# A three-layer graph network: the slot numbers of all node tiles scattered by GpSimd, and the second count of edges on TensorE taken out

## The reference

```python
h, residual = x, 0.0
for Wl, bl, Wr, g, b in params:
    s = segment_sum(h[src], dst, num_segments=N_NODES)
    cnt = segment_sum(ones, dst, num_segments=N_NODES)
    h = residual + (s / maximum(cnt, 1)) @ Wl.T + bl + h @ Wr.T
    h = prelu(layer_norm(h, g, b), a_prelu)
    residual = h
out = layernorm(x + h)
```

## Time and profile before

| what | value |
|---|---|
| median of 3 runs | 2023.56 us (2023.55 to 2024.12) |
| profiled execution, its own time | 2023.93 us |
| its span | 2022.1 us |
| mean granted TensorE clock | 0.993 of full speed |
| PE, DVE, ACT, POOL busy | 98%, 79%, 60%, 46% |
| data moved | 387.69 MB, mean 192 GB/s |

### The profile page before, as it was taken

One profiled execution on the slowest core, in us unless ns is written; L12 is line 12 of the kernel. 1 busy time (PEld: TensorE's weight loads), 2 busy tenths in 40 slices (PEclk: granted clock), 3 DMA queues, 4 the chain that ended last, 5 costly groups with the idle time before them and its releaser, 6 DMA issues. The chain is left out here.

```text
span 2022.1 us, 30522 instructions
## 1 busy us (share of the span) xinstructions
PE 1978.4 (98%) x10207; PEld 1659.0 (82%) x10207; DVE 1597.5 (79%) x2598; ACT 1221.7 (60%) x2667; POOL 926.7 (46%) x885
## 2 busy tenths in 40 slices
PE   8999999999999999999999999999999999999993
PEld 7888888888888888888888888887788888888882
DVE  7778777777777677777777777779999988888884
ACT  6865554554444455444444444458887777777774
POOL 3666656555565312332222333214555555555554
PEclk9999999999999999999999999999999999999997
DMA  6667667666666555544444444456666666656652
GB/s 209 226 232 258 215 219 233 221 208 214 204 204 207 161 162 183 170 146 152 146 145 151 157 156 144 138 173 216 221 230 217 211 212 213 209 203 218 214 183 92
DMA packets 181075, 387.69 MB, mean 192 GB/s; under 512 B 20117, under 2 KB 20562, under 8 KB 180918
## 3 DMA queue, kind: packets, MB, share of 16 engines
q1 hardware_dynamic: 142358, 272.06, 39.7%
q0 software_dynamic: 38560, 113.67, 17.3%
HBM read 221.07 MB, written 164.79 MB: 191 GB/s over the span
## 5 line engine op out<-in xcount | busy, mean ns | idle before, releaser
L411 PE MATMUL ps_z<-w_hi,hT_hi 128*128 128x512 f32 x1884 | 762.9, 405 | 5.7 <-ACT ps_z L553 4.9
L411 PE MATMUL ps_z<-w_hi,hT_lo 128*128 128x512 f32 x1884 | 738.6, 392 | 0.0
L411 PE MATMUL ps_z<-w_lo,hT_hi 128*128 128x512 f32 x1884 | 737.8, 392 | 0.0
L690 POOL TENSOR_TENSOR rstd<-veps,minus_half 128x2 f32<-128x2 f32 (+1 forms) x240 | 241.6, 1007 | 876.1 <-ACT veps L543 876.0
L790 DVE TENSOR_TENSOR hT_lo<-ps_t,hT_hi 128x1024 fp32r<-128x1024 f32 (+1 forms) x237 | 288.0, 1215 | 320.3 <-ACT hT_hi L524 317.6
L553 ACT COPY ps_z<-bias_rows 128x512 f32<-128x512 f32 x471 | 276.7, 588 | 346.5 <-DVE y L801 334.7
L533 ACT ACTIVATE junk<-ps_z 128x512 f32<-128x512 f32 x471 | 278.6, 592 | 322.3 <-PE ps_z L411 322.1
L411 PEld LDWEIGHTS ps_z<-w_hi,hT_lo 128*128 128x128 f32 x1884 | 353.4, 188 | 79.0
L411 PEld LDWEIGHTS ps_z<-w_hi,hT_hi 128*128 128x128 f32 x1884 | 354.4, 188 | 75.9 <-issue 8.1
L411 PEld LDWEIGHTS ps_z<-w_lo,hT_hi 128*128 128x128 f32 x1884 | 354.8, 188 | 66.9
L801 DVE SCALAR_TENSOR_TENSOR y<-ps_z,rstd,gain 128x512 f32<-128x512 f32 x471 | 330.2, 742 | 4.5 <-POOL rstd L690 4.5
(11 more groups left out here) (144 smaller groups left out, 1928.9 us busy)
## 6 DMA issues: line engine op xcount, KB each, us to landing
h_scratch<-hout SPq DMA_DIRECT2D x156, 512.0 KB, 3.7
hin<-h_scratch SPq DMA_DIRECT2D x156, 512.0 KB, 3.9
x_by_slot<-hin SPq DMA_DIRECT2D x78, 512.0 KB, 3.3
o_sb<-x_by_slot SPq DMA_DIRECT2D x78, 512.0 KB, 4.6
rowtab<-edge_row_table SPq DMA_DIRECT2D x60, 256.0 KB, 3.6
stage<-in_WrT SPq DMA_DIRECT2D x3, 1024.0 KB, 8.2
stage<-in_WlT SPq DMA_DIRECT2D x3, 1024.0 KB, 7.4
hin<-in_x,node_get POOLq DMA_INDIRECT x157, 3.8
```

Of the source, the lines that this page charges most:

```text
L411: mm = pe.matmul(acc, a[:, k, :], ww[:, k, :], start=False, skip_group_check=True, stop=stop and k == KC - 1 and a is a_lo)
L690: nc.gpsimd.tensor_tensor(rstd[(T - 1) % 2][:, at], veps[(T - 1) % 2][:, at], minus_half[:, at], ALU.pow).then_inc(rstd_done, 1)
```

## The change

The second count goes: `count_signs`, `sign_tile`, the second set of keys, the second table with its transposes, casts and two stores, and the semaphores `slot_stored` and `keys_known`. Instead GpSimd scatters the slot numbers of all 157 tiles. `slot_int` grows to NT columns. `PUT_SLOT` has a place for each of the 157: the 40 edge tiles as before, but for the last three (now T = 79, 78, 78, 78 for tiles 36 to 39), the others at T = 2 to 19, two at each edge triple (at the edge unit and the one after it), and 59 spread over T = 79 to 92. By step that is one scatter at each T from 2 to 21; 2 and 1 at each edge unit and the one behind it up to T = 51, and 2, 2 and 1 in the triples from 53 on; 5 at T = 78, 6 at T = 79, then 54 at T = 80 to 92 (4 each, 5 at 83 and 88). `find_source` runs five units ahead instead of six and waits for 157 scatters. TensorE's wait before the first message sums is for the first table and the row step; VectorE's first `carry` waits for `node_stored`. `shared_hi` and `shared_lo` become tiles of their own (48 bytes each), the lists of two keys become single tiles.

```diff
-        slot_int = sb("slot_int", [P, ET], I32)
+        slot_int = sb("slot_int", [P, NT], I32)
...
-        key = [sb(f"key{i}", [P, ET]) for i in range(2)]
-        key_int = [sb(f"key_int{i}", [P, ET], I32) for i in range(2)]
+        key = sb("key", [P, ET])
+        key_int = sb("key_int", [P, ET], I32)
         key_part = sb("key_part", [P, ET], I32)
-        key_hi = [sb(f"key_hi{i}", [P, ET]) for i in range(2)]
-        key_lo = [sb(f"key_lo{i}", [P, ET]) for i in range(2)]
+        key_hi, key_lo = sb("key_hi", [P, ET]), sb("key_lo", [P, ET])
...
-        shared_hi, shared_lo = key_hi[1][:, ET - SHARE:ET], key_lo[1][:, ET - SHARE:ET]
+        shared_hi, shared_lo = sb("shared_hi", [P, SHARE]), sb("shared_lo", [P, SHARE])
...
-        PLACES = EDGE_AT[1:HALF] + [T + i for T in EDGE_AT[HALF:len(edge_units)] for i in range(3)] + [UL, UL + 1, UL + 2]
-        PUT_SLOT = PLACES[:ET]
-        SRC_AHEAD = 6
+        ROW_SLOT, SRC_AHEAD = 1, 5
+        PLACES = [T for T in range(2, LEAD)] + [T + i for T in EDGE_AT[:len(edge_units)] for i in range(2)]
+        REST = range(UL, EDGE_AT[len(edge_units)] - SRC_AHEAD - 1)
+        LATER = NT - ET - len(PLACES)
+        PLACES += [REST[i * len(REST) // LATER] for i in range(LATER)]
+        EDGE_PLACES = (EDGE_AT[1:HALF] + [T + i for T in EDGE_AT[HALF:len(edge_units)] for i in range(3)]
+                       + [UL - 1, UL - 1, UL - 1])
+        PUT_SLOT = EDGE_PLACES[:ET] + PLACES
...
-                if T == TABLE_SLOT + 2:
-                    sp.wait_ge(table_done, 3)
-                    sp.dma_start(slot_dram[0:P * P, :].rearrange("(t p) c -> t (p c)", p=P),
-                                 table_int[:, 0, :]).then_inc(slot_stored, 16)
-                    sp.dma_start(slot_dram[P * P:NT * P, :].rearrange("(t p) c -> t (p c)", p=P),
-                                 table_int[0:NT - P, 1, :]).then_inc(slot_stored, 16)
...
-            def count_signs(i):
-                pe.wait_ge(split_out, i + 1)
-                begin, end = i == ET - SHARE, i == 2 * ET - SHARE - 1
-                pe.matmul(signs_a, ones_short[:], tiles_above[i % HB], start=begin, stop=end)
-                pe.matmul(signs_b, places_from[i % HB], tiles_above[i % HB], start=begin, stop=end).then_inc(counted, 1)
...
-            def sign_tile(t):
-                i = ET - SHARE + t
-                act.wait_ge(counted, i - HB + 1)
-                nc.scalar.activation(tiles_above[i % HB], tile_row, ACT.Sign, bias=key_hi[1][:, t:t + 1])
-                nc.scalar.activation(places_from[i % HB], place_row, ACT.Sign,
-                                     bias=key_lo[1][:, t:t + 1]).then_inc(split_out, 1)
...
+                for t in range(NT):
                     if T == PUT_SLOT[t]:
-                        if t == 0:
-                            pool.wait_ge(slot_stored, 32)
-                        if t % BATCH == 0:
+                        if t == ET:
+                            pool.wait_ge(count_read, 1)
+                        if t < ET and t % BATCH == 0:
                             pool.wait_ge(nodes_known, 2 + t // BATCH)
                         pool.indirect_dma_start(slot_dram, bass.IndirectOffsetOnAxis(node_put[:, t:t + 1], 0),
                                                 slot_int[:, t:t + 1], None,
...
-                if T == TABLE_SLOT:
-                    then(nc.vector.tensor_scalar(table[:], slot_no, total[:, 0:1], float(-EP // 2), ALU.add, ALU.add))
-                    dve.wait_ge(counted, 2 * ET - SHARE)
...
-                if T == TABLE_SLOT + 2:
-                    dve.wait_ge(table_turned, 2)
-                    nc.vector.tensor_copy(table_int[:, 0, :], ps_s[0][:, 0:P]).then_inc(table_done, 1)
-                    nc.vector.tensor_copy(table_int[0:NT - P, 1, :], ps_s[0][0:NT - P, P:2 * P]).then_inc(table_done, 1)
```

More of the change, by code:

```diff
@@ L213, in build_program @@
         NODE_SLOT = [2 + t if t < EARLY else EDGE_AT[(t - EARLY) // 2] + 1 + t % 2 for t in range(ET)]
-        PLACES = EDGE_AT[1:HALF] + [T + i for T in EDGE_AT[HALF:len(edge_units)] for i in range(3)] + [UL, UL + 1, UL + 2]
-        PUT_SLOT = PLACES[:ET]
[L216 to L219, removed]
-        SRC_AHEAD = 6
-        assert all(NODE_SLOT[t] < KNOWN_SLOT[t // BATCH] < PUT_SLOT[t] for t in range(ET)) and TABLE_SLOT + 3 < LEAD - 1 and PUT_SLOT[0] > TABLE_SLOT + 4
-        assert len(PUT_SLOT) == ET and PUT_SLOT[-1] + 2 < EDGE_AT[len(edge_units)] - SRC_AHEAD
+        ROW_SLOT, SRC_AHEAD = 1, 5
[6 more added lines that the diff above has]
+        PUT_SLOT = EDGE_PLACES[:ET] + PLACES
+        assert all(NODE_SLOT[t] < KNOWN_SLOT[t // BATCH] < PUT_SLOT[t] for t in range(ET))
+        assert len(PUT_SLOT) == NT and max(PUT_SLOT) < EDGE_AT[len(edge_units)] - SRC_AHEAD
         def stats(T):
@@ L433, in product_mean, with turn_table @@
                 mm3(ps_z[u.r2][:, j, :], sT_hi[j], sT_lo[j], 2 * u.l + 1, True).then_inc(z_ready, 1)
[L435 to L438, removed]
+            def turn_table():
+                pe.transpose(ps_s[0][0:ET, 0:P], table[:, 0:ET], ident[:]).then_inc(table_turned, 1)
             def idle_work(count):
@@ L908, in vector_program @@
             then(nc.vector.tensor_tensor(fcol[:], dcol[:], rank[:], ALU.subtract))
-            then(nc.vector.scalar_tensor_tensor(key[0][:], fcol[:], total[:, 0:1], apart[:], ALU.add, ALU.add))
-            split_key(0)
-            negate_key(key_hi[0][:, ET - SHARE:ET], key_lo[0][:, ET - SHARE:ET], shared_hi, shared_lo).then_inc(first_keys, 1)
+            then(nc.vector.scalar_tensor_tensor(key[:], fcol[:], total[:, 0:1], apart[:], ALU.add, ALU.add))
+            split_key()
+            negate_key(key_hi[:, ET - SHARE:ET], key_lo[:, ET - SHARE:ET], shared_hi[:], shared_lo[:]).then_inc(first_keys, 1)
             for i in range(ET - SHARE):
@@ L930, in vector_program @@
             dve.wait_ge(table_turned, 1)
-            nc.vector.tensor_copy(table_int[0:ET, 0, :], ps_s[0][0:ET, 0:P]).then_inc(table_done, 1)
-            then(nc.vector.tensor_tensor(key[1][:], dcol[:], apart[:], ALU.add))
-            split_key(1)
-            negate_key(key_hi[1][:], key_lo[1][:], key_hi[1][:], key_lo[1][:]).then_inc(keys_known, 1)
+            nc.vector.tensor_copy(table_int[0:ET, :], ps_s[0][0:ET, 0:P]).then_inc(table_done, 1)
             for T in range(-1, UNITS + 3):
@@ L988, in vector_program @@
                         find_edge_nodes(b)
-                if T == TABLE_SLOT:
-                    then(nc.vector.tensor_scalar(table[:], slot_no, total[:, 0:1], float(-EP // 2), ALU.add, ALU.add))
-                    dve.wait_ge(counted, 2 * ET - SHARE)
-                    for part_, scale in ((signs_a[:, 0:NT], -0.25), (signs_a[:, 1:NT + 1], -0.25),
-                                         (signs_b[:, 0:NT], 0.25), (signs_b[:, 1:NT + 1], -0.25)):
-                        then(nc.vector.scalar_tensor_tensor(table[:], part_, scale, table[:], ALU.mult, ALU.add))
-                    dve.wait_ge(node_stored, 16)
-                    nc.vector.memset(total[:], 0.0).then_inc(count_read, 1)
-                if T == TABLE_SLOT + 2:
-                    dve.wait_ge(table_turned, 2)
-                    nc.vector.tensor_copy(table_int[:, 0, :], ps_s[0][:, 0:P]).then_inc(table_done, 1)
-                    nc.vector.tensor_copy(table_int[0:NT - P, 1, :], ps_s[0][0:NT - P, P:2 * P]).then_inc(table_done, 1)
         with nc.Block() as block:
```

50 lines of the change are left out of this document (18 added, 32 removed).

## The result

The changed kernel takes 2052.01 us (median of 4 runs, 2048.63 to 2056.87), the kernel before 2023.55 (2023.43 to 2024.12): 1.0142 times as long, 95% interval 1.0119 to 1.0165. That is 28.5 us slower; the forecast was 7 us faster, and the time lies outside the range of 2008 to 2031.

What follows compares the result with a forecast made beforehand. TensorE, busy over 98% of the span, was taken to bound the kernel. 2023.9 - 6.1 - 12.5 + 11.5 = 2016.8 us profiled, the median 0.4 lower at 2016.4, range 2008 to 2031.

Steps and rivals of the forecast that it cites:

- DMA itself: Added scatters' transfers: 15,000 more 4-byte packets, the present 40 landing in 5.6 us median, priced at nothing.
- sign work and table: TensorE's list: sign matmuls of the second count give back 5.9 us, two table transposes 0.22, together 6.1 us.
- layout of w_hi0: Layer 0 weights move to a multiple of 64, matmul steps fall from 233 to 227.5 ns: 12.5 us gained.
- GpSimd in layer 1: 65 scatters at T = 78 to 92, one blocked by VectorE per unit, delay TensorE: 11.5 us lost.
- DMA in layer 1: Last scatter is put two units before find_source waits for it, so no cost: 0.
- GpSimd and DMA in layer 0: 58 added scatters stay inside 3.7 us of slack: price 0, or 1 us with the cover gone; DMA nothing.
- No layout gain: Rival: the 233 ns steps of layer 0 have another cause and stay, 2029 us; chance 0.18.
- POOL worse: Rival: two blockings a unit or slower puts on GpSimd in layer 1, 26 us lost, 2031 us; chance 0.10.
- VectorE held up by GpSimd: Rival: puts started ahead of L822 or L828 stop VectorE, 20 us more, 2036 us; chance 0.04.
- Hidden: Rival: scatters don't meet L822, layer 1 loses only 2 us, 2007 us; chance 0.10.

Runs made afterwards that it cites:

- experiment 3: Changed kernel with every slot number at a place of its own 64 bytes in slot_dram, same scatters: 2023.08 us, 0.9996 of the kernel before.
- experiment 7: Changed kernel with slot_dram places 16 bytes apart: 2029.27 us, 1.0027 of the kernel before.
- 4: Changed kernel with no scatters at T = 2 to 19, three at each edge triple instead, places of 4 bytes: 2034.56 us, 1.0054 of the kernel before.
- 8: Changed kernel, places of 4 bytes, scatters scheduled evenly (more in layer 0, fewer per unit in layer 1): 2065.84 us, 1.0197 of the kernel before.
- experiment 9: Kernel before with 224 unused bytes ahead of w_hi0, which then lies at 195968: 2011.25 us, 0.9938 of the kernel before.
- e1_pad: Kernel before with 32 unused bytes ahead of w_hi0, which then lies at 195776: 2015.3 us, 0.9957 of the kernel before.
- e5_pad96: Kernel before with 96 unused bytes ahead of w_hi0, which then lies at 195840: 2021.75 us, 0.999 of the kernel before.
- experiment 10: Changed kernel with places 64 bytes apart, even scatter schedule, w_hi0 at 196480, index arithmetic behind the first gathers: 2008.16 us, 0.9922 of the kernel before.
- experiment 6: Changed kernel with places 64 bytes apart and scatters spread evenly, at most three a unit in layer 1: 2017.54 us, 0.9968 of the kernel before.
- experiment 2: Changed kernel with 32 bytes added, so w_hi0 is back at 195744: 2061.29 us, 1.0189 of the kernel before.
- e12_all64: Kernel before with all weights, hT and sT moved by 64 bytes, their distances kept: 2023.86 us, 1.0001 of the kernel before.

## Why the prediction was wrong

**The step that failed** is, in its words, "DMA itself: 15,000 more packets of 4 bytes; the 40 there now land in 5.6 us median ... Nothing for both". The number itself was too high: the profile counts 32 more packets for each added scatter, 3744 in all (42304 against 38560 in GpSimd's queue). But what failed is that the count was priced and not where the packets write. The 40 scatters of before carry the nodes of the edge tiles. 5,000 edges at random have about 4,400 different destinations among 20,000 nodes, so the words of one tile lie some 18 bytes apart in `slot_dram`. The added ones carry nodes without edges, of which there are about 15,600: 128 of these lie in 164 places, some 5 bytes apart (both are estimates from these counts). I priced the second kind by the first. Shown by runs: the places alone, moved apart, end the idle time (experiments 3 and 7); less space brings the DMA share back step by step (0.70, 0.73, 0.83, 0.97 at 64, 16, 8 and 4 bytes); scatters moved elsewhere take the idle time along (4 and 8). Neither GpSimd's time (1040.9 us busy against 1036.0) nor the count of packets (184644 in both) differs much or at all between experiment 7 and the change. The 5.6 us that I had looked at are the landing time of the other kind of scatter. The second half of the step failed as well, at a smaller price: "the last is put two units before find_source waits for it", and POOL waited 6.1 us for it. What inside the DMA engines or the memory holds a packet for microseconds was not measured and stays open. One more thing is not separated: wider places also spread the whole table, from 80 KB to 161, 322 and 1286, so the size of the table could count beside the nearness of the words. The 40 wider-spaced scatters of before went to the same 80 KB without harm, but they were few.

The sum as it came out, against the profiled 2049.8 us:

| term | forecast | measured | from |
|---|---|---|---|
| sign work and table | -6.1 | -6.1 taken over | -6.3 in layer 0, see below |
| layout of w_hi0 | -12.5 | -12.5 | experiment 9 |
| GpSimd in layer 1 | +11.5 | +12.4 | T = 79 to 95 |
| DMA in layer 1 | 0 | +0.9 | T = 95 to 98, POOL's wait for the scatters |
| GpSimd and DMA in layer 0 | 0 | +31.5 | 668.4 - 655.5 for T = 1 to 79, and the 18.6 that should have been gained |
| profiled execution | 2016.8 | 2050.1 | 2023.9 and the five |

The 31.5 are what is left when the two gains are taken as forecast, so the table has to add up. Two figures check them. The windows gave 30.7 of idle and slow-clock time. And experiment 3, with the same scatters at the same steps, took 640.8 us for T = 1 to 79; less 4.1 for the layout (e1_pad 647.1 against e9_pad224 643.0) that is 636.7, and the changed kernel's 668.4 are 31.7 more. Experiment 7 gives 636.7 too (647.1 less 10.4, e5_pad96 against e9_pad224). Nearly all falls in T = 5 to 24: at T = 5 the changed kernel was 2.7 us ahead, at T = 23 it was 21.5 behind.

**The sign work.** The first units bore it out: two plain units of the changed kernel start at 50.17 and 56.53 us, 6.36 apart instead of 6.91, of which the layout is 0.12 and the signs 0.43. Two pairs of runs with weights at equal distances give the whole of it, for T = 1 to 79: 647.1 us with the signs and 640.8 without them (e1_pad and experiment 3), 653.4 and 647.1 (e5_pad96 and experiment 7). That is 6.3 us each time, with all the scatters of layer 0 in it, so "Price 0; with the cover gone, 1 us" for GpSimd in layer 0 held. The best version keeps only 3.1 us (experiment 9 against 10). Part of the rest went in single units, 6.83 and 7.25 us at T = 15 and 16, 6.96 at T = 81. Why is open: experiment 3 has the same scatters up to T = 21, and its units 15 and 16 take 6.39.

**The layout.** The size was right and so was the direction: 12.5 forecast and 12.5 measured. The rule, a multiple of 64, was wrong and came out right by luck, since 195712 is in the good place by the rule that the runs support. Steps of 233 and 227.5 ns were read correctly from the earlier trace rows. Matmuls N cycles apart, 213 ns, as the Trainium skill has it (TensorE: Matmul & The Clock Gate, "Step-by-step: what each phase is for"; with the fixed cost that the same section adds it is 216), appeared in no run: no two of these matmuls started less than 223 ns apart.

**GpSimd in layer 1.** Right mechanism and nearly right size: 6.85 us a unit with four scatters against 6.8 forecast, 8.16 with five against 8.03, and the loss gone when there are two or three (experiment 6).

**The rivals.** "No layout gain" is refuted by experiment 2. "POOL worse" named the right side but not the cause: GpSimd lost 12.4, not 26. "VectorE held up by GpSimd" is refuted by the changed kernel's trace: up to 815 us, 85 of the operations L788 and L794 started while an indirect DMA was already running on GpSimd, and they took 1.24 and 1.28 us in the mean, as the others did. In the timeline above L794 starts at 759.52, inside the scatter of 758.43. The Trainium skill's rule of the shared port (SBUF — State Buffer, "SBUF: two separate sides") was seen in one direction only: a scatter waits for VectorE's operation, and a running scatter doesn't hold VectorE. "Hidden" fell as well. No rival was about the DMA engines, and that was the gap: the busy share of 0.65 to 0.78 in the very stretch where I put 18 scatters was there to be read in the windows.

## What to carry to other kernels

Before adding small indirect writes, work out how far apart in memory the words of one transfer lie, not only how many there are: words some 5 bytes apart cost this kernel 31 us, the same words four times as far apart nothing that could be told in layer 0, and the remedy is a wider place for each. Look for the harm in the landing times of the other transfers and in the DMA share of the stretch. And look which line a landing time belongs to: a view of one tile mixes all transfers of it, those that write it and those that read it. And when an edit changes the list of small tiles, compare the step of the matmuls before and after: a shift of 32 bytes was worth 12.5 us here, as much as any other term.

## What the runs showed of the hardware

- Dense small writes hold up the other transfers: at 4 bytes apiece in nearly neighbouring places the DMA engines are 0.97 busy and move 190 GB/s; at 64 bytes they are 0.70 busy and move 238, with the same number of packets (38 to 130 us). The median packet keeps its 84 ns; 249 packets take over 1 us, against 9.
- The step of a 512-column matmul of this kernel goes with the distance between the place of its moving operand (weights) and its stationary one (h), modulo 256 bytes. hT and sT lie at 128. At a distance of 0 a plain unit takes 6.35 us, at 32 6.47, at 64 6.39, at 128 6.45 (e9_pad224, before, e1_pad, e5_pad96); the mean steps in layer 0 are 227.7, 233.2, 229.4 and 231.0 ns. That it is a distance rests on e12_all64, and the period on e9_pad224; the rule stands on these four distances alone.
- After 4.6 us without work TensorE ran at half its clock for the following 5 us: matmuls 430 ns apart, then 227.
- A scatter that starts 0.05 to 0.1 us behind a VectorE operation with two SBUF inputs mostly takes 2.02 us instead of 0.98, and VectorE's operation keeps its 1.23 us. In some units a scatter 0.04 or 0.05 us behind it gets through in 0.98, and the operation takes 1.30.
